# Expert tiles inside the macros of a state-space mixer on one core of Trainium2

## What is computed

```python
    xn = _layernorm(x, axis=-1)
    x = x + _L0_attn_ref(xn, ...) + _L0_ffn_ref(xn, ...)
```

```python
        logits = xt @ router_w + router_b
        probs = jax.nn.softmax(logits, axis=-1)
        gate = jnp.max(probs, axis=-1)
        idx = jnp.argmax(probs, axis=-1)
        ...
        y = gate[:, None] * e_out      # e_out: row of xt @ expert_w[idx] + expert_b[idx]
```

## Time and profile before

| | us |
|---|---|
| median of 3 runs | 1167.79 (1166.45 to 1168.86) |
| profiled execution | 1168.7 |
| its span, first to last instruction | 1166.9 |
| PE busy in it | 1047.6 (90%) |
| DVE busy | 1009.0 (86%) |
| ACT busy | 850.0 (73%) |
| POOL busy | 328.4 (28%) |
| mean granted TensorE clock | 0.953 of full |

### The profile page before, as it was taken

One profiled execution on the slowest core, in us unless ns is written; L12 is line 12 of the kernel. 1 busy time (PEld: TensorE's weight loads), 2 busy tenths in 40 slices (PEclk: granted clock), 3 DMA queues, 4 the chain that ended last, 5 costly groups with the idle time before them and its releaser, 6 DMA issues.

```text
span 1166.9 us, 25635 instructions
## 1 busy us (share of the span) xinstructions
PE 1047.6 (90%) x8826; PEld 823.5 (71%) x8826; DVE 1009.0 (86%) x1837; ACT 850.0 (73%) x1549; POOL 328.4 (28%) x353
## 2 busy tenths in 40 slices
PE   4862599667999999999999999999999999999896
PEld 2532477445888887877877788787788788788675
DVE  5849633349999999999999999999999999999962
ACT  3941222059888888888888888888888888888750
POOL 1305777101222222222222222222222222222230
PEclk9985699977999999999999999999999999999998
DMA  7968366424455544445454555454454444554440
GB/s 232 318 229 354 109 213 211 128 71 128 134 152 155 155 147 149 149 144 161 149 154 148 151 155 154 147 154 147 153 157 154 148 148 146 157 147 152 131 150 21
DMA packets 141014, 185.64 MB, mean 159 GB/s; under 512 B 19950, under 2 KB 101151, under 8 KB 139472
## 3 DMA queue, kind: packets, MB, share of 16 engines
q1 hardware_dynamic: 114608, 146.70, 37.0%
q0 software_dynamic: 15744, 26.23, 11.1%
q10 hardware_dynamic: 10528, 11.01, 2.8%
HBM read 75.99 MB, written 40.63 MB: 100 GB/s over the span
## 4 chain that ended last, share of the span: by engine, by line
DVE 53%; issue 15%; PE 7%; DMA 1%; ACT 1%; DVEq 1%; POOL 0%; SPq 0%; POOLq 0%; ACTq 0%
DVE conv L1156 14%; DVE att L1242 4%; DVE g L1260 3%; DVE decay L1189 3%; DVE prod L1215 3%; DVE prod L1214 3%; PE ps L821 3%; DVE prod L1225 3%; DVE prod L1224 3%; DVE o_tile L1275 2%; DVE phase L1181 2%; DVE state L1250 2%; DVE lam L1173 2%; DVE cown L1229 2%; DVE theta L1164 2%
## 5 line engine op out<-in xcount | busy, mean ns | idle before, releaser
L821 PE MATMUL ps<-xn_in,win 128*128 128x256 f32 x1152 | 292.0, 396 | 25.7 <-DMA xn_in<-xnT_d 15.5
L821 PEld LDWEIGHTS ps<-xn_in,win 128*128 128x128 f32 x1152 | 215.6, 196 | 57.2 <-issue 13.2
L1156 DVE SCALAR_TENSOR_TENSOR conv<-x_pre,col,conv 128x256 f32<-128x256 f32 x480 | 195.1, 477 | 17.4 <-ACT conv L988 17.4
L1313 POOL TENSOR_TENSOR state_in<-state,cin_s 128x256 f32<-128x256 f32 x56 | 45.0, 803 | 387.8 <-DVE state L1250 387.8
L946 PE MATMUL ps<-wout,g 128*128 128x256 f32 x512 | 125.8, 390 | 5.3 <-DVE o_tile L1275 4.6
L946 PEld LDWEIGHTS ps<-wout,g 128*128 128x128 f32 x512 | 96.2, 193 | 22.3 <-issue 9.0
L1332 POOL TENSOR_TENSOR rms<-ms,cst 128x1 f32<-128x1 f32 x64 | 46.8, 732 | 219.0 <-DVE ms L1267 219.0
L933 PEld LDWEIGHTS ps<-att,x_tok 128*64 128x64 f32 x1024 | 54.6, 136 | 49.6 <-issue 28.8
L642 DVE TENSOR_TENSOR r_tiles<-ps,r_expw 128x256 f32<-128x256 f32 x72 | 30.6, 424 | 63.7 <-issue 48.7
L988 ACT ACTIVATE conv<-ps,col 128x256 f32<-128x256 f32 x160 | 83.6, 571 | 0.0
L1242 DVE TENSOR_TENSOR att<-ps,cst 128x1024 f32<-128x1024 f32 x64 | 77.1, 1204 | 5.5 <-PE ps L906 5.5
(11 more groups left out here) (169 smaller groups left out, 2367.7 us busy)
## 6 DMA issues: line engine op xcount, KB each, us to landing
cin_s<-cin SPq DMA_DIRECT2D x128, 129.0 KB, 2.3
rep<-bc_d SPq DMA_DIRECT2D x128, 128.0 KB
grow_s<-grow SPq DMA_DIRECT2D x128, 128.0 KB, 2.1
bup_s<-bup SPq DMA_DIRECT2D x128, 128.0 KB, 2.0
cown_s<-cown SPq DMA_DIRECT2D x128, 128.0 KB, 2.6
expert_d<-r_tiles ACTq DMA_DIRECT2D x18, 512.0 KB, 3.4
xn_d<-r_tokens SPq DMA_DIRECT2D x16, 512.0 KB, 4.3
xnT_d<-r_turned SPq DMA_DIRECT2D x4, 2048.0 KB, 24.1
```

The source lines that it names most:

```text
L821: last = nc.tensor.matmul(dst, win[:, kt, n * P:(n + 1) * P], xn_in[b][:, kt, :], start=(kt == 0), stop=(kt == KT - 1))
L1156: nc.vector.scalar_tensor_tensor(conv[:, ct, :], x_pre[b][:, ct, tap:tap + MT], c("conv_w", ct * D_CONV + tap), conv[:, ct, :], ALU.mult, ...
```

## The change

- Routing stops at `slot_of`: the one-hot tables, the 64 matmuls and `token_of` go. Rows are put in expert order by writing them: POOL scatters each tile's rows to a new buffer `xs_d` by `slot_of`. Slots that no token fills must hold numbers, so SP first writes zeros to 16 tiles of `xs_d`, whose numbers it reads from a table (`empties`). The last 16 tiles of rows are still in SBUF and are scattered in the routing block; the other 48 are read back from `xn_d` (`sort_load`, 11 loads through four buffers) and scattered (`sort_rows`) during the filling of the mixer.
- `xnT_d` is stored by ACT's queue. Softplus of dt, the gate and the limit on the decay move into the routing block, with looser waits.
- The expert stage goes. The 72 tiles are computed in the mixer, four in each of iterations 1 to 18, by one input buffer, one transposed buffer, two weight buffers (weights and bias of the tile's expert, 384 KB per tile, loaded each time by SP) and the free half of PSUM bank 3 (`bank_u`).
- Macros 0 to 20 (`DIRECT` = 21) have no expert rows yet when they end: SP loads x alone for them. Their 42 tiles are added to the output late, four per iteration from 20 on: POOL gathers, ACT scales by the gate, POOL adds to `out` with an accumulating transfer. Macros 21 to 31 are as before.
- `x_skip` goes: ACT writes D x straight into PSUM (`back_seed`, eight steps of 128 columns per macro), and PE accumulates on it. `back_ms` moves from DVE to ACT. `xbc` has three buffers.
- The order of steps in each engine's loop is rewritten.
- The variant for large decays (not taken here) gets an expert block of its own, left out below.

```diff
+        KEPT = 4
+        ROUTED = 20
+        ASIDE = SLOT_TILES + EXPERTS
+        SORT, _row = [], 0
+        for _n in range(10):
+            SORT.append((_n % 4, _row, (5, 5, 4, 4)[_n % 4]))
+            _row += SORT[-1][2]
+        SORT.append((0, _row, TILES - KEPT * GROUP - _row))
...
+                    sp.wait_ge(empties_ready, 3)
+                    for n in range(2 * EXPERTS):
+                        to = sp.value_load(empties[0:1, n:n + 1], min_val=0, max_val=ASIDE + EXPERTS - 1)
+                        sp.dma_start(xs_d.rearrange("(n p) d -> p n d", p=P)[:, bass.ds(to, 1), :], zero_rows[:, None, :]).then_inc(sp_stored, 16)
+                    sp.wait_ge(sp_stored, 16 * 2 * EXPERTS)
...
+                    pool.wait_ge(sp_stored, 16 * 2 * EXPERTS)
+                    pool.wait_ge(rv, ROUTED)
+                    for t in range(TILES - KEPT * GROUP, TILES):
+                        rows_of = a_xn[(t // GROUP) % AHEAD][:, t % GROUP, :]
+                        pool.indirect_dma_start(xs_d, bass.IndirectOffsetOnAxis(ap=slot_of[:, t:t + 1], axis=0), rows_of, None).then_inc(kept_sorted, 16)
+                    pool.wait_ge(kept_sorted, 16 * KEPT * GROUP)
...
+        def sort_load(sp, n, rows_of):
+            b, at, w = SORT[n]
+            after(sp, sort_done[b], 16 * sort_before(n))
+            sp.dma_start(rows_of[b][:, 0:w, :], xn_d[at * P:(at + w) * P, :].rearrange("(t p) d -> p t d", p=P)).then_inc(sort_loaded[b], 16)
+
+        def sort_rows(pool, n, rows_of):
+            b, at, w = SORT[n]
+            pool.wait_ge(sort_loaded[b], 16 * (sum(1 for i, _, _ in SORT[:n] if i == b) + 1))
+            for i in range(w):
+                pool.indirect_dma_start(xs_d, bass.IndirectOffsetOnAxis(ap=slot_of[:, at + i:at + i + 1], axis=0), rows_of[b][:, i, :], None).then_inc(sort_done[b], 16)
+
+        def tile_load(sp, j, e_in, e_w):
+            b = j % 2
+            if j == 0:
+                for n in range(4):
+                    sp.wait_ge(sort_done[n], 16 * sort_count(n))
+            after(sp, tile_turned, j)
+            sp.dma_start(e_in, xs_d[j * P:(j + 1) * P, :]).then_inc(tile_loaded, 16)
+            e = sp.value_load(tile_expert[0:1, j:j + 1], min_val=0, max_val=EXPERTS - 1)
+            after(sp, tile_added, j - 1)
+            sp.dma_start(e_w[b].rearrange("p k d -> p (k d)"), w_tile[:, bass.ds(e, 1), :].rearrange("p o d -> p (o d)")).then_inc(tile_weights[b], 16)
+
+        def tile_turn(pe, j, e_in, e_ps):
+            pe.wait_ge(tile_loaded, 16 * (j + 1))
+            after(pe, tile_added, j)
+            for kt in range(KT):
+                last = nc.tensor.transpose(e_ps[:, kt * P:(kt + 1) * P], e_in[:, kt * P:(kt + 1) * P], ident)
+            last.then_inc(tile_turned, 1)
+
+        def tile_evacuate(act, j, e_xT, e_ps):
+            act.wait_ge(tile_turned, j + 1)
+            after(act, tile_mm, j)
+            nc.scalar.activation(e_xT, e_ps, ACT.Copy).then_inc(tile_evac, 1)
+
+        def tile_product(pe, j, e_xT, e_w, e_ps):
+            b = j % 2
+            pe.wait_ge(tile_evac, j + 1)
+            pe.wait_ge(tile_weights[b], 16 * (j // 2 + 1))
+            for kt in range(KT):
+                last = nc.tensor.matmul(e_ps, e_xT[:, kt * P:(kt + 1) * P], e_w[b][:, kt, :], start=(kt == 0), stop=(kt == KT - 1))
+            last.then_inc(tile_mm, 1)
+
+        def tile_bias(dve, j, e_w, e_ps, e_out):
+            b = j % 2
+            dve.wait_ge(tile_mm, j + 1)
+            after(dve, tile_stored[b], 16 * (j // 2))
+            nc.vector.tensor_tensor(e_out[b], e_ps, e_w[b][:, KT, :], ALU.add).then_inc(tile_added, 1)
+
+        def tile_store(sp, j, e_out):
+            b = j % 2
+            sp.wait_ge(tile_added, j + 1)
+            sp.dma_start(expert_d[j * P:(j + 1) * P, :], e_out[b]).then_inc(tile_stored[b], 16)
...
+            e_in, e_xT = spare[:, 0, :], spare[:, 1, :]
+            e_w, e_out = [spare[:, 2:5, :], spare[:, 5:8, :]], [spare[:, 8, :], spare[:, 9, :]]
+            PER, FIRST, LATE = 4, 2, 4
...
+            def late_tiles(m):
+                first = LATE * (m - DIRECT + 1)
+                return range(max(first, 0), min(first + LATE, TPM * DIRECT))
...
                 sp.wait_ge(m_ready, 3)
+                for n in range(4):
+                    sort_load(sp, n, rows_of)
...
                 for m in range(-BEFORE, MACROS):
+                    replicate(m + 1)
                     load_xn(m + 3)
+                    expert_store(m, 3)
                     stack_grow(m + 1)
+                    expert_load(m + 1, 1)
+                    stack_cin(m + 1)
+                    expert_load(m + 1, 2)
                     load_hidden(m + 3)
+                    stack_cown(m + 1)
+                    expert_store(m + 1, 0)
+                    expert_load(m + 1, 3)
+                    stack_bup(m + 1)
+                    expert_store(m + 1, 1)
                     load_dt(m + 3)
-                    stack_cin(m + 1)
-                    stack_bup(m + 1)
-                    stack_cown(m + 1)
+                    expert_store(m + 1, 2)
                     bounce(m + 2)
+                    load_x(m + 1, 0)
                     store(m, 0)
-                    replicate(m + 2)
+                    expert_load(m + 2, 0)
+                    load_x(m + 1, 1)
                     store(m, 1)
+                    for n in {-2: range(4, 7), -1: range(7, len(SORT))}.get(m, ()):
+                        sort_load(sp, n, rows_of)
...
+                nc.tensor.matmul(bank_y, ident, cst[:, 0:PAIRS * P], start=True, stop=True).then_inc(s["opened"], 1)
                 for m in range(-BEFORE, MACROS):
-                    back_update(m, 0)
+                    back_turn(m, 0)
+                    front_z_b(m + 1)
+                    back_y(m, 0)
+                    back_turn(m, 1)
+                    back_update(m, 0, 4, 4)
                     back_scores(m, 1)
+                    expert_turn(m + 1, 0, -1)
+                    back_out(m, 0)
                     front_turn(m + 1, 0)
+                    expert_product(m + 1, 0, -1)
                     front_x_a(m + 3)
+                    back_square_sum(m, 0)
+                    expert_turn(m + 1, 1, -1)
+                    front_x_b(m + 3)
+                    back_y(m, 1)
+                    expert_product(m + 1, 1, -1)
+                    front_x_c(m + 3)
+                    expert_turn(m + 1, 2, -1)
                     front_turn(m + 1, 1)
-                    front_x_b(m + 3)
-                    back_out(m, 0)
-                    back_y(m, 1)
-                    back_square_sum(m, 0)
-                    front_x_c(m + 3)
-                    back_update(m, 1)
                     front_theta(m + 3)
-                    back_turn(m + 1, 0)
+                    back_update(m, 1, 7, 6)
                     back_out(m, 1)
+                    expert_product(m + 1, 2, 0)
+                    back_square_sum(m, 1)
                     front_z_a(m + 2)
-                    back_square_sum(m, 1)
+                    expert_turn(m + 1, 3, 0)
                     back_scores(m + 1, 0)
-                    front_z_b(m + 2)
-                    back_y(m + 1, 0)
-                    back_turn(m + 1, 1)
+                    expert_product(m + 1, 3, 0)
...
+                def back_seed(m, ch):
+                    t = m * TPM + ch
                     act.wait_ge(s["silu"], m + 1)
-                    after(act, s["yout"], TPM * (m - 1))
+                    act.wait_ge(s["opened"], 1)
+                    after(act, s["gated"], t)
                     for q in range(PAIRS):
-                        last = nc.scalar.activation(x_skip[b][:, q, :], xbc[:, q, :], ACT.Copy, scale=c("D", q))
+                        last = nc.scalar.activation(bank_y[:, q * P:(q + 1) * P], xbc[m % XBC_BUFS][:, q, ch * P:(ch + 1) * P], ACT.Copy, scale=c("D", q))
                     last.then_inc(s["xd"], 1)
...
+                def late_scale(m):
+                    if late_tiles(m):
+                        act.wait_ge(late_in, 16 * late_tiles(m).stop)
+                        for t in late_tiles(m):
+                            last = nc.scalar.activation(spare[:, t % (2 * LATE), :], spare[:, t % (2 * LATE), :], ACT.Copy, scale=gate[:, t:t + 1])
+                        last.then_inc(s["lscaled"], 1)
...
+                    if m == 0:
+                        dve.wait_ge(sort_done[2 + ch], 16 * sort_count(2 + ch))
...
+                    back_gate(m, 0)
+                    front_phase(m + 2)
+                    back_state(m, 0)
+                    front_cin(m + 1)
+                    back_mask(m, 1)
+                    expert_bias(m + 1, 0)
+                    front_cown(m + 1)
+                    front_frac(m + 2)
+                    front_bup(m + 1)
+                    back_final(m, 0)
+                    expert_bias(m + 1, 1)
+                    back_gate(m, 1)
                     front_lamdt(m + 2)
```

(44 more changed lines are left out.)

628 lines of the change are left out of this document (344 added, 284 removed).

## The result

The changed kernel takes **1205.13 us** in the median of 4 runs (1202.65 to 1209.6), the kernel before 1168.32 beside it (1166.45 to 1169.02): ratio **1.0322, 95% interval 1.0295 to 1.0349**. It is slower by 3.2%; I had predicted 1139, faster, and gave slower 0.12. The profiled execution took 1209.6 us, its span 1207.8.

A forecast was written before the change was run, and what follows sets the result against it. PE and DVE were taken to be both full in the steady mixer (98.7% each), with PE setting the tile macros. Terms -98 + 22.4 + 46.3 + 1 = -28.3; 1168.7 - 28.3 - 0.9 = 1139.5, predicted 1139, range 1108 to 1168.

The forecast's parts named there:

- Routing and expert stage, -98: Before the mixer: routing ends with row numbers, the expert stage goes, so the mixer starts at 134.5 and not 232.5 us.
- zero write at 0.9: In routing: each of SP's 16 zero writes, value load and address included, takes 0.9 us; issued by 104, landed by 108.
- Filling, +22.4: Mixer's filling: macro 1's products start 86 us in, not 63.6; 14 us of this from SP's hold at sort loads.
- Tile macros, +46.3: Iterations 1 to 18, four expert tiles each: 30.1 us per macro and not 27.53.
- PE sets it: Tile macros: PE's 30.1 us sets the pace, above DVE's 28.7, ACT's 25.3 and SP's 25 to 26.4.
- Rival (a): Tile macros: PE has room, DVE paces them at 28.7 us; 25 us less, 1114; chance 0.13.
- Other macros, +1: The 12 macros without tiles: 27.6 us each, ACT at 26.6 just under DVE's 27.4, POOL 17 of 27 us.
- Tail unchanged: Behind the last mark: the late adds' last pair lands about where the last store does, so 44.9 us stay.
- (d): Tile macros: the `bup` stack comes late in every one, 32.0 us per macro, +34 us, 1173; chance 0.12.
- (e): Tile macros: tiles wait for each other through single `e_in` and PSUM half; 0.6 us a macro, 1150; chance 0.08.
- (b): Filling: SP is not held, as writes run faster or other work covers it; 14 us less, 1125; chance 0.17.
- (c): Routing and filling: indirect writes cost 2.26 us each; 16 us more first, 9 in the hold, 1164; chance 0.10.

The follow-up runs named there:

- e4: Changed kernel with SP issuing the replicating transfers of macro 1 ahead of sort loads 7 to 10; ratio 1.0263 to the kernel before.
- e6b: Changed kernel with all eleven sort loads issued by POOL between its scatters, none by SP; ratio 1.0268 to the kernel before.
- e11: Changed kernel with e2 in all macros, e3, e6b, e7, e9 and zero writes split over two queues; 1149.91 us, ratio 0.9832 to the kernel before.
- e2: Changed kernel with the replicating transfers of macro m+2 issued ahead of store(m, 1), from macro 0 on; ratio 1.0136 to the kernel before.
- e3: Changed kernel with expert stores and x loads moved from SP's queue to POOL's; ratio 1.0164 to the kernel before.
- e12: e11 with each tile's product cut to the first of its two halves; 1168.4 us on a chip where the kernel before takes 1182.1.
- e7: Changed kernel with POOL's late gathers behind the second root and late adds one macro later; ratio 1.0219 to the kernel before.
- e1: Changed kernel without the late share: no late gathers, scaling or accumulating transfers to the output; ratio 1.0015 to the kernel before.
- e9: Changed kernel with the untaken halved experts moved from their own block into the mixer's block; ratio 1.0305 to the kernel before.
- e13: e11 without the code of the halved experts, never taken on this data; ratio 0.9887 to the kernel before.
- e15: Kernel before without its halved mixer, whose branch is never taken, and that branch's block; 1179.1 us, the kernel before 1183.0 beside it.
- e14: Kernel before with one more block holding one untaken wait per engine; 1185.6 us, the kernel before 1183.0 beside it.

## Why the prediction was wrong

**Routing and expert stage, -98: right in kind, 5.3 short.** `slot_of` was ready at 92.8 (I said 94.6), 16 indirect writes took 1.26 us each (1.25) and landed after 2.4. The term that failed is the zero write at 0.9: they start 1.5 us apart, of which the issue is 0.33, so value load and address take 1.2 and not 0.56, which I had put together from DVE's 0.35. POOL's first scatter came at 115.04, not 108.

```profile
90.53 22.85 SPq L410 DMA_DIRECT2D xs_d<-r_tiles  x16
...
200.48 0.43 SPq L619 DMA_DIRECT2D att<-xn_d  x1
200.96 17.97 SPq L619 DMA_DIRECT2D spare<-xn_d  x3
219.04 2.58 SPq L784 DMA_DIRECT2D rep<-bc_d  x4
```

**Filling, +22.4: the number and the place were right** (85.3 us in, SP held 18 us ahead of `rep`; rows above). That it was worth "14 of it this hold" was not: e4 and e6b show two more holds under it, and what e6b wins by macro 1, 15.6 us, is 3.5 at macro 2.

**Tile macros, +46.3: 23.5 short.** The failed step is "PE sets it", with the SP sum of "25 to 26.4" treated as hidden beneath it. PE's 30.1 was a good count: 452.43 / 470 x 31.40 = 30.2 us busy, and the step is 30.21 with SP relieved in e11. SP's sum was short by the value loads, four of 0.83 us and not 0.35: it is 28.3. But I also took a sum below the macro for cover. An in-order queue of 28.3 us that also waits for cin, for turns and for the final puts its late transfers on DVE's path: 16.6 and 13.7 us of named waits in 470. e2 and e3 give back 0.55 and 0.8 of the 1.3, e11 with both 1.2. DVE was dearer too: 457.0 / 470 x 29.97 = 29.1, not 28.7.

Rival (a), that PE has room and DVE paces the tile macros at 28.7, did not come: no run has a tile step below 29.97. The runs leave less between it and my 30.1 than I thought: with PE cut by 1.7 us (e12) the macro still takes 29.97, so room on PE would have been worth 0.24 us a macro here. The weight loads stand at 375.84 of 470 us, 80% as before, and at 389.43, 83%, in e11 with PE's rows at 99.0%. The Trainium skill, Perfetto Trace Analysis, section Identifying the Most-Contended Engine, says to judge PE's headroom by that share (and by the share of peak arithmetic). With DVE full as well, these runs cannot say whether PE had the 17% of room that this share leaves.

**Other macros, +1: the largest miss, 33.5.** The failed step is the one from the busy sums ("17 of 27 us" for POOL, "ACT stands at 26.6") to 27.6: it has no term for what stands behind what in a queue. The change moved `replicate` behind `store(m, 1)`, and put four gathers of 1.3 to 3.9 us ahead of the root that this store waits for. e7 undoes one (-1.2), e2 the other (-0.7), e11 both: 27.71, near my 27.6. Engine counts gave the floor; the order of two queues kept the kernel 2.7 us above it. (That ACT would be next was not so: in e11 it works 24.6 us of a late macro and not 26.6, and DVE sets the 27.71.) I had read `replicate` behind the last x load in the filling and named what it held there, and did not ask the same of the thirty macros that follow.

**"Tail unchanged": 7.7 short.** The late adds, which I had weighed, cost nothing there (e1). The extra block at the end had no term in my sum. Behind the last store's issue 10.7 us more pass with no engine at work, in front of it 3.0 less. Of the 10.7, 4.7 go with the extra block (e9) and 1.3 more with its untaken code (e13); 4.7 stay open.

**The rivals.** (d), the only slower one, was wrong in its place: PE has no wait for `bup_s` between 330 and 800 us. Its kind, a transfer late in SP's queue, was right, for `rep` and `dt_in`. (e) is there in part: PE waits 5.7 us in 470 for a bias before a turn, 0.4 a macro of the 0.6 that I gave it. (b) and (c) did not happen, (a) is told above. I had written that I am wrong in kind if SP has no gaps. It has 2.65 us of them in 30.95, and the miss was of that kind.

## What to carry to other kernels

A count per engine gives a floor. Where a queue kept in order comes within a few microseconds of that floor, or stands behind a step at the iteration's end, walk it row by row: for each transfer that an engine waits for, ask what wait now stands ahead of it, and what has to end before that. When work is spread into a steady loop, recheck its critical transfer (here `rep`) in every kind of iteration, not only where the change is. And a hold that is removed gains only up to the next one under it: read the mark after the next.

## What was unexpected

- A value load on SP leaves 0.76 to 0.87 us between two transfers of a tile macro. On DVE the gap was 0.35.
- Code that is not taken costs time at the end: 5.2 us for the kernel's long halved mixer with its block (e15 against before), with no engine at work.
- Chips differ, and not evenly. On the chip of e14 and e15 the kernel before ran its mixer at the same 27.5 us a macro, but the mixer started at 247.58 and not 232.31 (e15). POOL's 72 indirect reads of the expert stage, last two idle reasons (us, times) in e15:

```profile
  issue: 19.2, 63
  remote: 16.6, 7
```

In the first profile of before there is no such "remote" wait, a release whose sender the profile does not show. It is not the indirect reads' alone: in the same profile ACT and DVE wait 48.9 and 36.5 us under this name, all in the expert stage. Every profile from a chip on which the kernel before takes 1182 us or more has such waits, and none from one with 1168. What causes them is open. A kernel without the expert stage is spared these, which fits with e1 to e4 looking 1% better. But e13, which is e11 less code that is never taken, gives 0.9887 on such a chip and e11 0.9832 on the other. The late macros differ: e12's eleven, on that chip, take 19 us more than e11's, and DVE's "remote" waits in them, up to 3.1 us each, are 11.8 of these. So a ratio depends on the chip, by 0.5 to 1% and either way, and only a control on the same chip, or the marks of the trace, can tell that from an effect.
